# Attention projection and 1x1 maps of a convolution and attention kernel: plain fp32 on parts of the TensorE array in place of three fp32r products on all of it

## What is computed

```
for _ in range(3):
    t = relu(conv3x3(x, w1) + b1)
    x = x + 1/3 * (conv3x3(t, w2) + b2)
x = relu(x)

qkv = einsum('oc,bchw->bhwo', qkv_w, x)          # 8 heads of 8 channels
k = ln(k); v = ln(v)                             # over the 8 channels of a head
kv = einsum('bhnd,bhne->bhde', k, v) / N
ret = einsum('bhnd,bhde->bhne', q, kv) + x
u = gelu(einsum('oc,bchw->bohw', o1_w, ret))
out = gelu(einsum('oc,bchw->bohw', o2_w, u) + x)
```

## Time and profile before

| what | us |
|---|---|
| median of 2 runs | 1665.46 |
| lowest and highest run | 1665.19, 1665.73 |
| the profiled execution, its own time | 1664.34 |
| its span in the trace | 1662.2 |

### The profile page before, as it was taken

The page is one execution under the profiler, slowest core; times in us unless marked ns, Lnnn a source line. Parts: engine busy times, 40 slices in busy tenths (PEclk is TensorE's granted clock), DMA queues, the critical chain, the costliest instruction groups (busy, mean ns, idle before and its releaser), DMA issues.

```text
span 1662.2 us, 25169 instructions
## 1 busy us (share of the span) xinstructions
PE 1616.9 (97%) x8955; PEld 1465.4 (88%) x8955; DVE 1219.9 (73%) x2275; ACT 783.5 (47%) x1386; POOL 85.7 (5%) x107
## 2 busy tenths in 40 slices
PE   7999999999999999999999999999999999999966
PEld 6899999899988899989998899988999889998864
DVE  5665787677777776877777779677687767876775
ACT  4333644447443564345644455443554446444444
POOL 0000000000000000000000000000000000000000
PEclk9999999999999999999999999999999999999988
DMA  6212231323412233123411252123421231213212
GB/s 111 51 26 51 51 58 33 64 51 53 77 26 51 51 67 62 26 51 65 89 26 37 52 91 52 26 39 64 78 51 31 52 68 30 39 29 61 51 26 51
DMA packets 149190, 85.97 MB, mean 52 GB/s; under 512 B 136652, under 2 KB 136652, under 8 KB 149068
## 3 DMA queue, kind: packets, MB, share of 16 engines
q0 software_dynamic: 13824, 50.34, 16.8%
q1 hardware_dynamic: 135164, 33.82, 11.1%
q10 hardware_dynamic: 80, 0.15, 0.0%
HBM read 17.17 MB, written 16.78 MB: 20 GB/s over the span
## 4 chain that ended last, share of the span: by engine, by line
PE 87%; DVE 7%; issue 3%; ACT 3%; DMA 0%; ACTq 0%; SPq 0%; DVEq 0%
PE bank L974 27%; PE bank L933 17%; PE bank L935 17%; PE bank L934 16%; PE bank L1023 3%; PE bank L1011 2%; PE bank L1013 2%; PE bank L1012 2%; ACT t_eo L503 1%; DVE y L865 1%; DVE v_all L754 1%; DVE y L868 1%; ACT x_hi L529 0%; DVE g_lo L851 0%; DVE rstd L817 0%
## 5 line engine op out<-in xcount | busy, mean ns | idle before, releaser
L933 PE MATMUL bank<-x_hi,w_hi 128*128 128x448 f32 (+2 forms) x1440 | 518.6, 360 | 3.5 <-DVE x_lo L664 3.3
L974 PE MATMUL bank<-v_all,fw 128*128 128x256 f32 x2304 | 515.4, 381 | 4.0 <-DVE v_all L754 4.0
L935 PE MATMUL bank<-x_hi,w_lo 128*128 128x448 f32 (+2 forms) x1440 | 509.5, 354 | 0.0
L934 PE MATMUL bank<-x_lo,w_hi 128*128 128x448 f32 (+2 forms) x1440 | 508.8, 353 | 0.0
L974 PEld LDWEIGHTS bank<-v_all,fw 128*128 128x128 f32 x2304 | 432.1, 190 | 68.7 <-ACT m L516 5.5
L933 PEld LDWEIGHTS bank<-x_hi,w_hi 128*128 128x128 f32 x1440 | 272.3, 189 | 21.9 <-issue 5.0
L934 PEld LDWEIGHTS bank<-x_lo,w_hi 128*128 128x128 f32 x1440 | 271.9, 189 | 15.3
L935 PEld LDWEIGHTS bank<-x_hi,w_lo 128*128 128x128 f32 x1440 | 271.7, 189 | 15.2
L503 ACT ACTIVATE t_eo<-bank,b_col 128x384 f32<-128x384 f32 (+2 forms) x240 | 141.4, 589 | 292.0 <-PE bank L935 291.4
L516 ACT ACTIVATE m<-bank 128x512 f32<-128x512 f32 x192 | 114.2, 601 | 152.0 <-PE bank L974 152.0
L739 DVE TENSOR_TENSOR steps_q<-t_eo 128x1344 f32<-128x1344 f32 x96 | 119.9, 1249 | 80.3 <-ACT t_eo L503 80.3
(11 more groups left out here) (131 smaller groups left out, 1989.8 us busy)
## 6 DMA issues: line engine op xcount, KB each, us to landing
x_res<-dx POOLq DMA_DIRECT2D x96, 512.0 KB, 4.6
x_in<-in_x SPq DMA_DIRECT2D x64, 256.0 KB, 6.9
out<-y_out SPq DMA_DIRECT2D x120, 128.0 KB, 2.6
out<-v_all SPq DMA_DIRECT2D x8, 128.0 KB, 2.7
x_res<-in_L_conv_w ACTq DMA_DIRECT2D x1, 144.0 KB, 3.2
x_res<-in_L_conv_w SPq DMA_DIRECT2D x1, 144.0 KB, 4.8
b_col<-in_L_conv_b SPq DMA_DIRECT2D x4, 0.2 KB, 2.9
g<-in_L_conv_o_w SPq DMA_DIRECT2D x3, 16.0 KB
```

What stands on the lines that cost most here:

```text
L933: mm(ps, lhs[0], rhs[0], start=first, stop=False)
L934: mm(ps, lhs[0], rhs[1], start=False, stop=False)
L935: return mm(ps, lhs[1], rhs[0], start=False, stop=last)
L974: last = mm(ps, fw[:, q, 1 - stack, :], v_all[:, KEPT.index(q), g0 + stack:g0 + stack + size, :], start=stack == 0, stop=stack == 1)
```

## The change

PROJECT, UP and DOWN multiply in plain fp32 and don't use the split. A matmul is given only the partitions of one half: 64 rows of the array by 128 columns in PROJECT, 64 by 64 in UP and DOWN. The program issues two ring uses at a time, each bank of the pair being written by one half of the rows (PROJECT: bank 0 gets the even rows of pixels, bank 1 the odd ones; UP and DOWN: four matmuls, one for each combination of a row half and a column half). The weight tiles `kvw`, `gw` and `o2` no longer have zero blocks. Before the first matmul of a pair the PE waits for both banks of the ring, and increments a semaphore that nobody waits for (`tiles_begun`).

The passes that made the low parts are gone: `f_lo`, `g_lo`, `gw_lo`, the second GELU, the second addition after DOWN, and the zeroing of the weight tiles. DOWN waits for the GELUs of both of its inputs. In `LATE` and `LAST` the two members of a pair stand at the place of the later one; all other pieces stay where they were.

```diff
@@ the table of places; LAST is changed in the same way
-        (PROJECT, 0, (2, 2, 3, 3, 3, 4, 4, 6)), (DEVIATION, 0, (3, 6)), (INVERT, 0, (3, 7)),
+        (PROJECT, 0, (2, 2, 3, 3, 4, 4, 6, 6)), (DEVIATION, 0, (3, 6)), (INVERT, 0, (3, 7)),
...
-        (OUTER, 1, (21, 23, 23, 23, 23, 24, 27, 27)), (UP, 0, (22, 23, 25, 26)), (DOWN, 0, (23, 24, 27, 28)),
+        (OUTER, 1, (21, 23, 23, 23, 23, 24, 27, 27)), (UP, 0, (23, 23, 26, 26)), (DOWN, 0, (24, 24, 28, 28)),
@@ ScalarE, the ReLU and UP
-                    nc.scalar.activation(f_hi[img][:, at], x_res[img][:, at], ACT.Relu).then_inc(hi_written, 1)
+                    nc.scalar.activation(f[img][:, at], x_res[img][:, at], ACT.Relu).then_inc(f_written, 1)
...
-                            act.wait_ge(g_split, done - 1)
-                            act.wait_ge(down_ready, done - 1)
+                            act.wait_ge(down_ready, done - k % 2)
                         ps = ring_ps[uses.index(s) % RING]
-                        nc.scalar.activation(g[k % 2][:, :], ps[:, :], ACT.Gelu)
-                        nc.scalar.activation(g_hi[k % 2][:, :], ps[:, :], ACT.Gelu).then_inc(gelu_done, 1)
+                        nc.scalar.activation(g[k % 2][:, :], ps[:, :], ACT.Gelu).then_inc(gelu_done, 1)
@@ VectorE, UP and DOWN
-                    elif kind == UP:
-                        dve.wait_ge(gelu_done, tail + 1)
-                        vec.tensor_tensor(g_lo[k % 2][:, :], g[k % 2][:, :], g_hi[k % 2][:, :].bitcast(F32),
-                                        ALU.subtract).then_inc(g_split, 1)
...
-                        vec.tensor_tensor(y[k % 2][:, :], ps[:, :], f_hi[img][:, at].bitcast(F32), ALU.add
-                                        ).then_inc(f_hi_added, 1)
-                        dve.wait_ge(f_hi_added, tail + 1)
-                        vec.tensor_tensor(y[k % 2][:, :], y[k % 2][:, :], f_lo[img][:, at].bitcast(F32), ALU.add
+                        vec.tensor_tensor(result(img, k, uses is RING_LAST), ps[:, :], f[img][:, at], ALU.add
                                         ).then_inc(down_added, 1)
@@ TensorE
+            def ring_pair(a, kind, img, k, uses):
+
+                first, second = (releaser(a, (kind, img, k + j), uses) for j in range(2))
+                if second:
+                    pe.wait_ge(*second)
+                if first and first[0] is not second[0]:
+                    pe.wait_ge(*first)
+                return [ring_ps[uses.index((kind, img, k + j)) % RING] for j in range(2)]
...
                     if kind == PROJECT:
-                        ps = ring_free(a, s, uses)
-                        for j in range(PER_BANK):
-                            at = slice(P * (PER_BANK * k + j), P * (PER_BANK * k + j + 1))
-                            to = ps[:, 2 * KV * j:2 * KV * (j + 1)]
-                            mm(to, f_hi[img][:, at], kvw_hi[:, :], start=True, stop=False)
-                            mm(to, f_hi[img][:, at], kvw_lo[:, :], start=False, stop=False)
-                            last = mm(to, f_lo[img][:, at], kvw_hi[:, :], start=False, stop=True)
-                        last.then_inc(proj_ready, 1)
+                        if k % 2:
+                            continue
+                        both = ring_pair(a, kind, img, k, uses)
+                        pe.sem_inc(tiles_begun, 1)
+                        for j in range(PX_BANK):
+                            at = slice(P * (PX_BANK * (k // 2) + j), P * (PX_BANK * (k // 2) + j + 1))
+                            for p, ps in enumerate(both):
+                                rows = slice(CH * p, CH * p + CH)
+                                last = mm(ps[:, KV * j:KV * (j + 1)], f[img][rows, at], kvw[rows, :],
+                                          start=True, stop=True)
+                                if j == PX_BANK - 1:
+                                    last.then_inc(proj_ready, 1)
...
                     elif kind == UP:
-                        three(ring_free(a, s, uses)[:, :], (gw_hi[img][:, :], gw_lo[img][:, :]),
-                              (f_hi[img][:, at], f_lo[img][:, at]),
-                              True, True).then_inc(up_ready, 1)
+                        both = ring_pair(a, kind, img, k, uses)
+                        pe.sem_inc(tiles_begun, 1)
+                        for j in range(2):
+                            to = slice(CH * j, CH * j + CH)
+                            at = slice(BANK * (k + j), BANK * (k + j + 1))
+                            for p, ps in enumerate(both):
+                                rows = slice(CH * p, CH * p + CH)
+                                last = mm(ps[to, :], gw[img][rows, :], f[img][rows, at], start=True, stop=True)
+                                if j == 1:
+                                    last.then_inc(up_ready, 1)
                     elif kind == DOWN:
-                        pe.wait_ge(g_split, tail + 1)
+                        pe.wait_ge(gelu_done, tail + 2)
...
+                        for p in range(2):
+                            to = slice(CH * p, CH * p + CH)
+                            for j, ps in enumerate(both):
+                                rows = slice(CH * j, CH * j + CH)
+                                last = mm(ps[to, :], o2[rows, :], g[p][rows, :], start=True, stop=True)
```

More of the change, by code:

```diff
@@ L158 @@
         + steps(PROJECT, 1, 6, 7) + steps(NORMALISE, 1, 1) + steps(DEVIATION, 1, 1)
[L159 to L168, removed]
+        + steps(NORMALISE, 1, 2) + steps(INVERT, 1, 1) + steps(UP, 0, 0, 1)
+        + steps(NORMALISE, 1, 3) + steps(OUTER, 1, 0, 1, 2, 3) + steps(NORMALISE, 1, 4, 5) + steps(DOWN, 0, 0, 1)
+        + steps(NORMALISE, 1, 6) + steps(UP, 0, 2, 3) + steps(FINISH, 0, 0) + steps(NORMALISE, 1, 7)
+        + steps(OUTER, 1, 4, 5, 6, 7) + steps(FINISH, 0, 1) + steps(FOLD, 1, 0, 1) + steps(DOWN, 0, 2, 3)
+        + steps(FINISH, 0, 2) + steps(FOLD, 1, 2, 3) + steps(UP, 1, 0, 1) + steps(FINISH, 0, 3)
+        + steps(DOWN, 1, 0, 1) + steps(UP, 1, 2, 3) + steps(FINISH, 1, 0, 1) + steps(DOWN, 1, 2, 3)
+        + steps(FINISH, 1, 2, 3))
 def ring_uses(todo):
@@ L215, in conv_attention_kernel @@
         dx = pair_of("dx", [P, HALF_PX])
-        f_hi = pair_of("f_hi", [P, PIX], F32R)
-        f_lo = pair_of("f_lo", [P, PIX], F32R)
+        f = pair_of("f", [P, PIX])
         kv = sb("kv", [P, BLOCKS * 2 * 2, ONE])
@@ L699, in set_up @@
                     link(vec.tensor_scalar(kvw_mean, kvw_sum, 1.0 / HD, None, ALU.mult))
-                    link(vec.tensor_tensor(kvw_centred.rearrange("p (h d) -> p h d", d=HD), heads,
+                    link(vec.tensor_tensor(kvw.rearrange("p (h d) -> p h d", d=HD), heads,
                                          kvw_mean.rearrange("p (h a) -> p h a", a=1).broadcast_to([P, KV // HD, HD]),
                                          ALU.subtract))
[L703 to L708, removed]
+                    vec.tensor_copy(o2[:, :], banks[7][:, KV:KV + CH])
                     vec.tensor_copy(o1_t[:, :], banks[7][0:CH, KV + CH:KV + 2 * CH]).then_inc(weights_split, 1)
@@ L981, in bank_free, with releaser @@
                     pe.wait_ge(drained, i * NU + unit - CONV_BANKS + 1)
[L983 removed]
+            def releaser(a, s, uses):
                 r = uses.index(s)
[L986 to L995 removed]
+                if r < RING and not (isinstance(a, int) and a > 0):
+                    return None
+                kind, img, k = uses[r - RING] if r >= RING else RING_USES[r - RING]
+                b = a if r >= RING else a - 1
+                if kind == PROJECT:
+                    return proj_taken, b * 2 * PROJ + img * PROJ + k + 1
+                if kind == UP:
+                    return gelu_done, b * 2 * TAILS + img * TAILS + k + 1
+                return down_added, b * 2 * TAILS + img * TAILS + k + 1
+            def ring_pair(a, kind, img, k, uses):
[5 more added lines that the diff above has]
+                return [ring_ps[uses.index((kind, img, k + j)) % RING] for j in range(2)]
             def attention(a, todo, uses):
@@ L1044, in attention @@
                     elif kind == UP:
+                        if k % 2:
+                            continue
                         if k == 0:
                             pe.wait_ge(small_taken, a * 10 + img * 5 + 5)
-                        at = slice(BANK * k, BANK * (k + 1))
-                        three(ring_free(a, s, uses)[:, :], (gw_hi[img][:, :], gw_lo[img][:, :]),
-                              (f_hi[img][:, at], f_lo[img][:, at]),
-                              True, True).then_inc(up_ready, 1)
-                    elif kind == DOWN:
-                        pe.wait_ge(g_split, tail + 1)
-                        three(ring_free(a, s, uses)[:, :], (o2_hi[:, :], o2_lo[:, :]),
-                              (g_hi[k % 2][:, :], g_lo[k % 2][:, :]),
-                              True, True).then_inc(down_ready, 1)
+                        both = ring_pair(a, kind, img, k, uses)
```

(11 more changed lines are left out.)

69 lines of the change are left out of this document (17 added, 52 removed).

## The result

The changed kernel takes 1622.06 us (two runs, 1621.86 and 1622.26) against 1665.46 us: a ratio of 0.974 with a 95% interval of 0.970 to 0.978, 43 us faster. A later comparison on another chip gave 1625.27 against 1665.49 us, 0.9757 (0.9738 to 0.9776). The forecast was 1655 us in a range of 1614 to 1724; the time lies in the range and at rival 1, which stood at 1625.

The account below looks back on a forecast made before the run. The prediction took the PE's matmul steps as the bound up to 1500 us. PROJECT -36.9, UP and DOWN -6.6, crossings +39.2 and tail -6 gave -10.3 us, 1654.0 on the profiled execution, forecast 1655 us, range 1614 to 1724.

Parts of the forecast that it names:

- rival 1: In PROJECT, UP and DOWN, all four parts run freely: 0.864 us per UP pair, 1625 us in all; chance 0.24.
- What bounds the kernel: Up to 1500 us the time is the sum of the PE's steps; after that the engines wait for one another.
- The overlap of the parts: In UP and DOWN, halves run side by side, column parts overlap partly: 3 steps of 0.432 us per pair, -6.6 us.
- The point of 3.2 steps: At UP, the steps per pair above which the group was to cost more than before.
- PROJECT's: In PROJECT, each half does its 8 records in 8 x 0.108 = 0.86 us per pair: -36.9 us.
- rival 3: The parts' weight loads don't overlap: PROJECT takes 1.73 us per pair, +18.4 us, 1710 us in all; chance 0.08.
- Rival 2: Matmuls start in program order over all parts, only neighbours overlap: 2.16 us per UP pair, 1720 us; chance 0.27.
- The crossing: Into and out of each group between whole-array matmuls, about 0.35 us are lost: 112 round trips, +39.2 us.
- The waits of the pairs: PE waits for two ring banks, and in DOWN two GELUs: costed at 0, at most 12 us.
- In the loop they hide behind the PE and are worth 0: The passes removed from VectorE and ScalarE save nothing in the loop.
- The tail: After 1560 us, removed passes and copies leave the chain: -6 us, -9 with full overlap of the parts.

Follow-up runs that it names:

- the whole array: The changed kernel with 128-row weights and zero blocks, so every plain fp32 matmul of PROJECT, UP and DOWN uses the whole array: 1682.85 us.
- one half: The changed kernel with every PROJECT, UP and DOWN matmul reading the lower 64 partitions: 1735.87 us.
- the padding: The changed kernel with three small FOLD matmuls padded with zeros to 65 by 65 and 65 by 128: 1610.01 us.
- the kernel in twos: The changed kernel with PROJECT's eight matmuls ordered two on the lower half, two on the upper, and the same again: 1627.84 us.
- with the passes back: The changed kernel with f_lo, g_lo, the second addition after DOWN and the second GELU put back as work nobody needs: 1641.37 us.

## Why the prediction was right, and where it was not

The result lies in the range because the range reached down to rival 1. The forecast itself, 10 us off the kernel before where 43 came off, took the wrong one of two overlaps: it had 0.33 of the chance and rival 1 had 0.24.

- **What bounds the kernel** was right: before and after, the PE waits under 3 us in the loop, and where an experiment changed the PE's steps and left the places, the time followed (the whole array +61 us for 62, one half +112 for 111, the padding -15 for 15).
- **The overlap of the parts** is the term that was mis-sized. The step was "Per half this gives for UP: first record, then second record beside the first of the other column half, then its second: 3 steps of 0.432". It is 2 steps: 1.02 us with drain, not 1.30 and its drain. For UP and DOWN that makes 64 x 0.432 = 27.6 us, nearly all of the 33 us between forecast and result. What ties the parts together is the order of issue, and it reaches further than I took it: up to three records may wait for a busy part, and four parts with two records each never fill that. The point of 3.2 steps from which a group was to cost more than before also left out the crossing: with 0.36 us of it, a pair pays only below (1.40 - 0.36)/0.432 = 2.4 steps, so for a pair that stands alone the 3 steps of the forecast would have been a loss.
- **PROJECT's** 8 steps per half held, at 0.112 us each and not 0.108 (0.89 per pair). That weight loads of the two halves don't overlap (rival 3) is refuted by it: 16 loads fit in 0.89 us.
- **Rival 2**, starts in program order over all parts, needed 2.16 us per UP pair and gave 1720 us. It is refuted by the 1.02 us. The rule of the Trainium skill that was named beside it, "TensorE: Matmul & The Clock Gate", Part 3, strict order of the matmuls' starts, doesn't hold between parts here: in the kernel in twos the upper half's first record, which belongs to the third matmul, starts before the first record of the second matmul, and with the rule eight records of 0.432 us wouldn't fit in 1.02 us. The measurement decides.
- **The crossing** of 0.35 us held: 0.36 at DOWN, 0.32 by the padded FOLD matmuls, and 0.40 at the two PROJECT pairs shown ((645.37 - 0.21) - (642.80 + 0.18) = 2.18 us, less 2 x 0.89). Its cause, only argued from one row before, is shown by the whole-array kernel (no loss with the same waits) and by the padding (the loss goes with the 65th row). That the array has to drain is what the Trainium skill says ("TensorEngine Tiling (Array Packing)", Key Properties); the runs show the price and what it hangs on, not the drain.
- **The waits of the pairs**, taken as 0, don't show: all of the PE's waits listed from 200 to 1460 us are 0.6 us, for `v_all`.
- **"In the loop they hide behind the PE and are worth 0"** was wrong. That cover held at 200.6 us per iteration, not at 196.6: with the passes back, `v_all` comes late and an iteration takes 1.2 us more, 8 us in all. I had compared VectorE's sum of 1100 us with the span, but within one pass over an image VectorE stands in the PE's chain whatever its sum. It didn't spoil the sum, since the passes really left.
- **The tail**, -6 (or -9 with full overlap), was 10.1 us. With the idle passes back it is 9.2 longer, so nearly all of it is the passes.
- With full overlap the sum of the prediction is 1625 us, from the same rows; the measured 1622 differs by 3, of which the tail is 1. The choice between the overlaps, not the prices, was the error.

The best version is the changed kernel with padded FOLD matmuls, 1610 us, 0.967 of the kernel before.

## What to carry to other kernels

Before splitting a matmul over parts of the array, count the crossings: each group paid 0.36 us here, so a group worth 1.4 us before and 0.86 after is left with a third of what the arithmetic says. Look also for small matmuls of 64 rows or columns or fewer that stand alone between whole-array ones: padding three of them by one row or column gave 15 us, a third of the whole change again. And an engine that is at 67% may still hold up the bound one within a stage; put its removed work back as idle work to see what its removal was worth.

## What the runs showed of the hardware that I had not expected

- Four 64 by 64 parts overlapped fully with two records each, and two column parts of one row half did as well (1.88 us for 8 records of 0.432).
- The reach of issue is short: with 8 records to one half ahead of the other, the other began 0.55 us late, with the fifth; with 4 ahead it began 0.014 us late. That fits three waiting records per busy part. It isn't three in all: in a DOWN group all four second records have begun their loads, at 744.59 to 744.61, before any of them starts. No run tells whether other shapes reach further.
- In the kernel in twos, what broke a half's stream of records cost more than it seemed: its next record started with its load not done ahead, and the one after it came 0.21 us later instead of 0.11.
- A matmul with 64 rows or 64 stationary columns is treated as a part even when nothing runs beside it, and one zero row or column more takes 0.3 us off.
